# Context attention: the value products of the preceding chunk between the two halves of a slot

## The chip, the cores and the metric

The kernel runs on one core of a Trainium2 chip, in one launch. The metric is the device time in microseconds; of several runs the median is given. The core has five engines with an instruction queue each: PE (TensorE, the matmuls), ACT (ScalarE), DVE (VectorE), POOL (GpSimd) and SP (SyncE, which here only issues transfers). They meet through semaphores alone.

## The reference

A small transformer block on a batch of 2. `ctx` has 77 rows of 512 values, `x` has 2048; 16 heads of 32 values, relative position biases in every attention, layer norms with scale and bias:

```
mem = ctx + mha(ln(ctx), ln(ctx));   mem = mem + ffn(ln(mem))            # 77 rows, small
y = x + mha(ln1(x), ln1(x), causal + bias)                               # self attention, 2048 rows
y = y + mha(ln2(y), mem, bias)                                           # context attention: 2048 queries, 77 keys
out = y + relu(ln3(y) @ w1.T + b1) @ w2.T + b2                           # feed-forward, width 2048
```

with `mha = softmax(q k' / sqrt(32) + bias) v`, then an output projection. All is float32. The kernel splits the operands of the large products into a high and a low part and adds three products (high high, high low, low high).

## The kernel before, in words

The stages follow one another: projections and the small context part, self attention, its output with the context queries, **context attention** (`cross_attention`, line 1369), feed-forward (`feed_forward`). Each is a block with one program for each engine; the next begins when all engines have left it.

In context attention the 4096 tokens are 8 groups of 512 tokens. A **chunk** q is 4 heads (128 of the 512 query columns) of one group, so there are 32 chunks (NQ); `q // 4` is the group and `q % 4` the set of heads. A chunk has 4 tiles of 128 tokens; tile n is `4 q + i`. For a chunk the work is:

- `score(n)`, PE, line 1505: three matmuls, 128 queries by 4 x 77 keys, into one of three PSUM banks `ca_s`; it waits until the exponentials three tiles back are done. The first score of a chunk waits for the chunk's queries.
- `shift(n)`, DVE: the negated maximum of each head (`ca_ng`, line 1642), with a bias added first (line 1640) for a few tiles near the start of each batch.
- `exponent(n)`, ACT, line 1582: four exponentials into `ca_pq`; `sums(n)` (line 1647) and `inverse(n)` (line 1652, two tiles at once) on DVE; the normalising multiplication on POOL (line 1484), two tiles at a time.
- `turn(q, j)`, PE, line 1519: four transposes of head j into one of two banks `ca_t`; the first head waits for POOL's normalising of each of the four tiles. `evacuate(q, j)`, ACT, line 1590, copies them to `ca_pt`, of which there are two, by the chunk's parity.
- `values(q)`, PE, line 1528, operation `ca_o` of line 1533: the **value products**, four matmuls of 77 x 32 by 512 (eight in the profile) into the one bank `ov`. Two waits stand ahead of them: for the four copies of chunk q, and for `low(q - 1)`, which frees the bank.
- `high(q)`, ACT, line 1596 (written as `sa_q`, which lends its room), and `low(q)`, DVE, line 1657 (`sa_k`): the two parts of the result.
- `project(e, ...)`, PE, line 1537, operation `ca_p` of line 1547: the output projection of tile e (128 tokens, all heads) in two halves of six matmuls. The first half waits for `low` of all four chunks of the tile's group. `residual(e)`, DVE, line 1662, adds it to `y`, and SP stores `y`.

The order of the work is written out by hand: every engine walks through the same slots, q from -2 to 36. In **slot** q PE works on `turn` of chunk q, `score` of chunk q + 2, `project` of tile q - 5 and `values` of chunk q - 1. All but the last is in two halves. ACT does `high(q - 2)` first in a slot, then in each half two copies and two tiles' exponentials; DVE does `low(q - 2)` first, then in each half two shifts, two sums of the tiles before, an inverse, and in half 0 the residual of tile q - 6. As tile e is projected in slot e + 5, the first tile of a group (e = 4, 8, ...) comes in slots 9, 13, ..., and needs `low` of chunk e + 3, which DVE does in that same slot.

POOL, in slot q: two pairs of normalisings, the bias row added to a `y` tile (line 1491), and one piece of later weights loaded, rounded and split (lines 173, 179, 181); in slot 5 also a memset (line 1498). In slot 29 DVE does the statistics of the feed-forward stage's first layer norm ahead of its shifts (`head_stats`), and in slot 30 ACT its square root ahead of its copies; PE transposes the result at the end of slot 32 (`head_turn`).

PE's part of the slot in the kernel before:

```python
            for q in slots():
                e = q - LAG
                for half in range(2):
                    ...
                    if has(e, NE):
                        project(e, (2 * half, 2 * half + 1))
                if has(q - 1):
                    values(q - 1)
                if q == NQ:
                    head_turn()
```

Of the kernel before, what the change touches and what calls it, by code (L numbers as in the profile page):

```python
# [152 lines left out]
def waits(engine, sem, value):  # L153

    if not (isinstance(value, int) and value <= 0):
        engine.wait_ge(sem, value)
# [1212 lines left out]
def cross_attention(k, io, dr, ident, w, split, src, dst, early, pair, stored, w2):  # L1369
# [7 lines left out]
    with k:  # L1377
# [26 lines left out]
        def slots():  # L1404
            return range(-LEAD, NQ + LAG)

        def chunk(q):
            return q // KC, q % KC, q // KC // GB
# [8 lines left out]
        def has(q, count=NQ):  # L1417
            return 0 <= q < count
# [84 lines left out]
        @block.tensor  # L1503
        def _(pe):
            def score(n):
                q, i = n // TT, n % TT
                g, m, b = chunk(q)
                if i == 0:
                    waits(pe, s[f"q{q % QB}"], 16 * (q // QB + q % QB // 2))
                    if q == NQ // B:  # L1510
                        pe.wait_ge(s["key1"], 16 * 2 * HC)
                waits(pe, s["exp"], n - 2)
                t = slice(i * P, (i + 1) * P)
                for x, (a, c) in enumerate(((0, 0), (0, 1), (1, 0))):
                    last = pe.matmul(sps[n % 3][:, 0:W], qb[q % QB][:, a, t], kd[b][:, c, m, :],
                                     start=(x == 0), stop=(x == 2))
                last.then_inc(s["score"], 1)

            def turn(q, j):
                n = q * HC + j  # L1520
                waits(pe, s["copied"], n - 1)
                for i in range(TT):
                    if j == 0:
                        pe.wait_ge(s["normal"], TT * q + i + 1)
                    last = pe.transpose(tps[n % 2][0:S, i * P:(i + 1) * P], pq_rows[(TT * q + i) % (PB * TT)][:, j, :], ident[:])
                last.then_inc(s["turned"], 1)

            def values(q):
                g, m, b = chunk(q)
                pe.wait_ge(s["copied"], HC * (q + 1))  # L1530
                waits(pe, s["low"], q)
                for j in range(HC):
                    last = pe.matmul(ov[j * HD:(j + 1) * HD, :], cv[:, b, m * HC + j, 0:HD], pt[:, q % 2, j, :],
                                     start=True, stop=True)
                last.then_inc(s["value"], 1)

            def project(e, cs):
                g, i = e // TT, e % TT
                if cs[0] == 0:
                    if e == 0:  # L1540
                        pe.wait_ge(split.s["lo"], KC)
                    pe.wait_ge(s["low"], KC * (g + 1))
                    waits(pe, s["done"], e - 1)
                t = slice(i * P, (i + 1) * P)
                for c in cs:
                    for x, (a, ww) in enumerate(((oh, wo_h), (oh, wo_l), (ol, wo_h))):
                        last = pe.matmul(ops[e % 2][:], a[g % 2][:, c, t], ww[:, c, :],
                                         start=(c == 0 and x == 0), stop=(c == KC - 1 and x == 2))
                if cs[-1] == KC - 1:
                    last.then_inc(s["product"], 1)  # L1550

            def head_turn():
                pe.wait_ge(s["normed"], TT)
                for c in range(KC):
                    for i in range(TT):
                        last = pe.transpose(banks[c][:, i * P:(i + 1) * P], xn0[:, i, c * P:(c + 1) * P], ident[:])
                    last.then_inc(s["across"], 1)
# [4 lines that stand above are left out]
                    if has(q):  # L1562
                        for j in (2 * half, 2 * half + 1):
                            turn(q, j)
                    if has(q + LEAD):
                        for i in (2 * half, 2 * half + 1):
                            score(TT * (q + LEAD) + i)
                    if has(e, NE):
                        project(e, (2 * half, 2 * half + 1))
                if has(q - 1):  # L1570
                    values(q - 1)
                if q == NQ:
                    head_turn()

# [657 lines left out]
```

## Time and profile before

| | us |
|---|---|
| median of 3 runs | 2810.82 (2808.09 to 2813.54) |
| the profiled execution | 2810.91 |
| its span, first to last instruction | 2808.8 |
| context attention, PE's first score to its last projection | 1819.99 to 2078.6 |
| PE busy over the span | 2705.2 (96%) |
| mean granted clock of TensorE | 0.987 |

Times in the trace count from the span's start. PE, ACT, DVE and POOL are the engines' work; PEld is PE's loading of weights, which runs beside its matmuls. A row of a timeline gives the start, the time that the merged instructions take together, the engine, the line, the operation with the tiles that it writes and reads, how many there are, and in brackets the idle time of the engine before it with what ended it. A matmul's end is modelled, so two rows of PE may overlap by some tenths; starts are what to go by. Slot 24 starts at 2003.83, slot 5 at 1862.09 and slot 7 at 1878.32.

### The profile page before, as it was taken

To read this page: it belongs to the slowest core of one execution; us is meant where nothing else is said; L and a number is where in the kernel's file an instruction comes from. 1 tells how busy PE (TensorE), PEld (TensorE's weight loads), DVE (VectorE), ACT (ScalarE), POOL (GpSimd) and SP (SyncE) were. 2 spreads that over 40 slices of the span, in tenths; PEclk is the share of its full clock that TensorE was granted. 3 is DMA by queue.
4 is the path that set the end of the run, shared out by engine and by line. 5 is a ranking of instruction groups with operands and counts; after the bars stand their busy time and mean duration, and the time that the engine had idled before them with its cause. 6 is when DMAs were issued, how large, how long until landed. Compare 5 with 4: busy or idle time off the path is not lost. (4 is left out here: it accounts for less than half of the span.)

```text
span 2808.8 us, 40054 instructions
## 1 busy us (share of the span) xinstructions
PE 2705.2 (96%) x12704; PEld 1794.2 (64%) x12704; DVE 1602.1 (57%) x3851; ACT 1238.1 (44%) x2624; POOL 417.4 (15%) x497
## 2 busy tenths in 40 slices
PE   7999989999999999999999889889999999999998
PEld 6788854444444444444444378767778888888886
DVE  5554367777777777777777288567643222122211
ACT  2322114555555555555555433488843323332231
POOL 5000021000000000000000422088557000000000
PEclk9999988999999999999999999999999999999999
DMA  7656653222222222222222388455431000000000
GB/s 222 220 187 207 196 155 80 69 68 67 69 69 69 69 70 69 69 68 62 58 60 49 101 219 255 179 178 181 154 115 40 31 30 31 30 0 30 31 16 16
DMA packets 138949, 272.96 MB, mean 97 GB/s; under 512 B 24885, under 2 KB 56117, under 8 KB 133498
## 3 DMA queue, kind: packets, MB, share of 16 engines
q1 hardware_dynamic: 133530, 255.14, 31.5%
q0 software_dynamic: 5216, 15.33, 1.9%
q8 instruction: 101, 1.65, 0.2%
q14 instruction: 102, 0.84, 0.1%
HBM read 176.02 MB, written 99.98 MB: 98 GB/s over the span
## 5 line engine op out<-in xcount | busy, mean ns | idle before, releaser
L1277 ACT ACTIVATE sa_pr<-sa_st 128x512 f32<-128x512 f32 (+3 forms) x1280 | 611.0, 532 | 538.2 <-DVE sa_st L1340 294.7
L1243 PE MATMUL sa_ov<-sa_pr,sa_v 128*33 128x512 f32 (+3 forms) x2560 | 535.8, 540 | 0.0
L1324 DVE TENSOR_REDUCE sa_part<-sa_mp 128x1 f32<-128x512 f32 x760 | 408.3, 584 | 115.0 <-PE sa_mp L1222 114.4
L1232 PE MATMUL sa_st<-sa_q,sa_k 97*128 97x512 f32 (+3 forms) x1280 | 441.7, 413 | 18.2 <-ACT sa_pr L1277 13.7
L1232 PEld LDWEIGHTS sa_st<-sa_q,sa_k 97*128 97x128 f32 x1280 | 217.0, 190 | 319.7 <-ACT sa_pr L1277 214.3
L1222 PE MATMUL sa_mp<-sa_k,sa_q 96*128 96x512 f32 (+1 forms) x1256 | 362.3, 382 | 10.6 <-PEq L1204 5.5
L1321 DVE CUSTOM_DVE_ANT_0 sa_mp<-sa_mp,sa_ub 128x512 f32<-128x512 f32 (+1 forms) x496 | 308.4, 665 | 76.9 <-PE sa_mp L1222 75.0
L148 PE MATMUL ff_f<-sa_q,ff_w 128*128 128x512 f32 x1024 | 336.5, 390 | 2.9 <-PEq L2039 2.9
L2034 PE MATMUL ff_o<-ff_w,ca_q 128*128 128x512 f32 x1280 | 330.2, 392 | 3.6 <-DVE ca_q L2085 3.6
L2085 DVE TENSOR_TENSOR ca_q<-ca_v,ca_q 128x512 fp32r<-128x512 f32 x128 | 95.8, 749 | 379.5 <-ACT ca_q L2069 379.5
L1243 PEld LDWEIGHTS sa_ov<-sa_pr,sa_v 128*33 128x33 f32 x2560 | 122.2, 111 | 256.6 <-issue 208.2
L1222 PEld LDWEIGHTS sa_mp<-sa_k,sa_q 96*128 96x128 f32 x1256 | 225.9, 192 | 76.1 <-DVE sa_part L1324 23.3
L2034 PEld LDWEIGHTS ff_o<-ff_w,ca_q 128*128 128x128 f32 x1280 | 238.3, 188 | 55.2 <-DVE ca_q L2085 3.7
L2066 ACT ACTIVATE ca_v<-ff_f,ff_b 128x512 f32<-128x512 f32 x128 | 87.8, 686 | 381.7 <-PE ff_f L148 381.7
L1340 DVE TENSOR_TENSOR sa_st<-sa_st,sa_tb 128x256 f32<-128x256 f32 (+1 forms) x608 | 206.2, 381 | 75.6 <-PE sa_st L1232 74.2
L148 PEld LDWEIGHTS ff_f<-sa_q,ff_w 128*128 128x128 f32 x1024 | 192.3, 188 | 43.1 <-PEq L2039 3.3
L148 PE MATMUL ff_f<-sa_k,ff_w 128*128 128x512 f32 x512 | 199.5, 390 | 0.0
L1193 POOL TENSOR_TENSOR sao_ot<-sao_ot,sao_rb 128x512 f32<-128x512 f32 x8 | 10.2, 1272 | 1135.5 <-DMA sao_rb<-scratch_inv 1135.5
L1582 ACT ACTIVATE ca_pq<-ca_s,ca_ng 128x77 f32<-128x77 f32 x512 | 117.6, 342 | 21.9 <-DVE ca_ng L1642 21.7
L148 PEld LDWEIGHTS ff_f<-sa_k,ff_w 128*128 128x128 f32 x512 | 96.2, 188 | 19.9
L148 PE MATMUL qkv_ring<-sa_k,qkv_w 128*128 128x512 f32 x384 | 96.8, 405 | 4.4 <-DVE sa_k L271 3.6
L148 PE MATMUL sa_qps<-sa_ln_hi,ca_wq 128*128 128x512 f32 x256 | 87.8, 412 | 10.4 <-DVE sao_qst L1954 10.4
(239 smaller groups left out, 3283.7 us busy)
## 6 DMA issues: line engine op xcount, KB each, us to landing
sa_q<-scratch_q SPq DMA_DIRECT2D x96, 256.0 KB, 7.6
sa_k<-scratch_k SPq DMA_DIRECT2D x96, 256.0 KB, 8.6
scratch_q<-sao_qst SPq DMA_DIRECT2D x32, 512.0 KB, 4.2
ca_q<-scratch_q SPq DMA_DIRECT2D x32, 512.0 KB, 4.3
scratch_q<-sa_q SPq DMA_DIRECT2D x28, 512.0 KB, 7.8
scratch_k<-sa_q SPq DMA_DIRECT2D x28, 512.0 KB, 5.5
sa_v<-scratch_v SPq DMA_DIRECT2D x16, 528.0 KB, 13.5
scratch_o<-sa_osb SPq DMA_DIRECT2D x128, 66.0 KB
```

The lines of the kernel that those rows point to most:

```text
L148: last = pe.matmul(out, s, m, start=(k == 0), stop=(k == n - 1))
L1222: pe.matmul(mp[a % 2][:, h, 0:w], qs[n.par][rows, h, qb * P:(qb + 1) * P], ks[n.par][rows, h, k0:k0 + w], start=True, stop=True).then_inc( ...
L1232: pe.matmul(st[bank(u, h)][:, 0:w], ks[n.par][:, h, kb * P:(kb + 1) * P], qs[n.par][:, h, g * GW + c0:(g + 1) * GW], start=True, stop=True ...
L1243: last = pe.matmul(ov[64 * h:64 * h + VW, c0:GW], vs[n.par][:, kb, h, :], pr[:, u % 4, h, 0:GW - c0], start=(u in opens), stop=(u in ends))
L1277: act.activation(pr[:, u % 4, h, 0:w], st[bank(u, h)][:, 0:w], ACT.Exp, scale=SCALE).then_inc(s["exp"], 1)
L1321: dve.tensor_tensor_reduce(tile, tile, ub[n.par][:, h, GW - w:GW], 1.0, NEG, ALU.add, ALU.max, to)\
L1324: dve.tensor_reduce(to, tile, AX_X, ALU.max).then_inc(s["red"], 1)
L1340: dve.tensor_tensor(tile, tile, tb[n.par][:, h, t0:t0 + w], ALU.add).then_inc(s["bias"], 1)
L1582: last = act.activation(pq_rows[r][:, j, :], sps[n % 3][:, j * S:(j + 1) * S], ACT.Exp, bias=ng[:, r, j:j + 1])
L2034: last = pe.matmul(ops[i][:], a[:, f % 2, t], b[f], start=(f == 0 and n == 0), stop=(f == FC - 1 and n == 2))
L2066: act.activation(hf[:, f % 2, :], fps[f % 2][:], ACT.Relu, bias=b1[:, f:f + 1]).then_inc(s["relu"], 1)
L2085: dve.tensor_tensor(hl[:, f % 2, :], hf[:, f % 2, :], raw(hh[:, f % 2, :]), ALU.subtract)\
```

## The change

In PE's program of context attention, `values(q - 1)` stands inside the loop over the two halves, and is issued in half 0 alone, after that half's turns, scores and projection. The programs of the other engines, the waits and the instructions themselves are the same.

```diff
@@ -1567,8 +1567,8 @@
                             score(TT * (q + LEAD) + i)
                     if has(e, NE):
                         project(e, (2 * half, 2 * half + 1))
-                if has(q - 1):
-                    values(q - 1)
+                    if half == 0 and has(q - 1):
+                        values(q - 1)
                 if q == NQ:
                     head_turn()
```

## Rows read from the trace of the kernel before

**Rows 1.** The page, part 1: busy time of each engine, share, instructions.
```profile
PE 2705.2 (96%) x12704; PEld 1794.2 (64%) x12704; DVE 1602.1 (57%) x3851; ACT 1238.1 (44%) x2624; POOL 417.4 (15%) x497
```
**Rows 2.** The page, part 4: lines of the chain that ended last.
```profile
PE ff_o L2034 13%; PE ff_f L148 12%; PE ff_ln_tp L251 0%; DVE ff_y L2090 0%; DVE sa_v L2090 0%; DVE ca_q L2085 0%; DVEq L72 0%; DVEq L319 0%; PEldq L2039 0%; DVEq L2084 0%; DVEq L2089 0%; PEldq L2017 0%; PEldq L215 0%; PEldq L214 0%
```
**Rows 3.** Stretches: length, busy PE, PEld, DVE, ACT, POOL, then clock, DMA, GB/s.
```profile
1829.00:1834.00 5.00, 2.20 (x9) 1.91 (x10) 0.96 (x3) 2.31 (x9) 4.92 (x7) 0.50 0.95 339
...
1845.00:1862.00 17.00, 14.92 (x105) 10.35 (x105) 12.00 (x32) 16.47 (x59) 15.17 (x22) 1.00 0.42 132
...
1871.00:2041.00 170.00, 170.00 (x1109) 131.24 (x1108) 118.08 (x284) 144.86 (x484) 123.71 (x155) 1.00 0.52 166
```
**Rows 4.** Timeline of PE, slot 24 and the start of slot 25.
```profile
2003.83 1.10 PE L1525 MATMUL ca_t<-ident,ca_pq 128*77 128x128 f32 x8
...
2005.62 0.64 PE L1547 MATMUL ca_p<-ca_wo,sa_q 128*128 128x512 f32 x2
...
2007.02 1.03 PE L1525 MATMUL ca_t<-ident,ca_pq 128*77 128x128 f32 x8
2007.81 1.09 PE L1515 MATMUL ca_s<-ca_k,ca_q 128*128 128x308 f32 x6
...
2010.20 1.07 PE L1533 MATMUL ca_o<-ca_pt,ca_v 77*32 77x512 f32 x8
2011.20 0.99 PE L1525 MATMUL ca_t<-ident,ca_pq 128*77 128x128 f32 x7
```
**Rows 5.** Timeline of ACT in the same slot.
```profile
2009.03 1.83 ACT L1582 ACTIVATE ca_pq<-ca_s,ca_ng 128x77 f32<-128x77 f32 x8 [0.30 <-DVE ca_ng L1642]
2011.34 0.60 ACT L1596 ACTIVATE sa_q<-ca_o 128x512 fp32r<-128x512 f32 x1 [0.47 <-PE ca_o L1533]
```
**Rows 6.** Timeline of DVE in the same slot.
```profile
2008.52 0.90 DVE L1642 TENSOR_REDUCE ca_ng<-ca_s 128x4 f32<-128x308 f32 x2 [0.65 <-PE ca_s L1515]
...
2011.97 0.69 DVE L1657 TENSOR_TENSOR sa_k<-ca_o,sa_q 128x512 fp32r<-128x512 f32 x1 [1.55 <-ACT sa_q L1596]
```
**Rows 7.** Timeline of all engines, end of slot 4 and slot 5.
```profile
1862.07 1.84 ACT L1582 ACTIVATE ca_pq<-ca_s,ca_ng 128x77 f32<-128x77 f32 x8
...
1863.72 0.67 ACT L1596 ACTIVATE sa_q<-ca_o 128x512 fp32r<-128x512 f32 x1
...
1864.43 0.69 DVE L1657 TENSOR_TENSOR sa_k<-ca_o,sa_q 128x512 fp32r<-128x512 f32 x1 [1.75 <-ACT sa_q L1596]
...
1865.27 0.69 PE L1547 MATMUL ca_p<-ca_wo,sa_q 128*128 128x512 f32 x2 [1.22 <-DVE sa_k L1657]
```
**Rows 8.** Timeline of all engines, slots 3 and 4.
```profile
1852.25 0.69 DVE L1657 TENSOR_TENSOR sa_k<-ca_o,sa_q 128x512 fp32r<-128x512 f32 x1 [1.75 <-ACT sa_q L1596]
...
1852.75 1.15 PE L1525 MATMUL ca_t<-ident,ca_pq 128*77 128x128 f32 x8 [0.85 <-ACT ca_pt L1590]
...
1857.63 0.67 ACT L1596 ACTIVATE sa_q<-ca_o 128x512 fp32r<-128x512 f32 x1
```
**Rows 9.** Timeline of all engines, slots 5 to 7: POOL's queue and PE's turns.
```profile
1870.21 1.36 POOL L1484 TENSOR_TENSOR ca_pq<-ca_pq,ca_inv 128x308 f32<-128x308 f32 x2 [1.06 <-DVE ca_inv L1652]
...
1875.26 2.15 POOL L1498 MEMSET ca_k<- 128x2464 f32 x1
...
1877.38 2.66 POOL L1484 TENSOR_TENSOR ca_pq<-ca_pq,ca_inv 128x308 f32<-128x308 f32 x4
...
1878.32 1.23 PE L1525 MATMUL ca_t<-ident,ca_pq 128*77 128x128 f32 x8
```
**Rows 10.** Timeline of all engines, slots 15 and 16.
```profile
1942.01 1.36 POOL L1484 TENSOR_TENSOR ca_pq<-ca_pq,ca_inv 128x308 f32<-128x308 f32 x2
...
1944.77 1.10 PE L1525 MATMUL ca_t<-ident,ca_pq 128*77 128x128 f32 x8
```
**Rows 11.** Timeline of PE, slots 29 and 30.
```profile
2046.61 0.69 PE L1515 MATMUL ca_s<-ca_k,ca_q 128*128 128x308 f32 x3 [1.25 <-ACT ca_pq L1582]
...
2052.59 1.15 PE L1525 MATMUL ca_t<-ident,ca_pq 128*77 128x128 f32 x8 [0.52 <-ACT ca_pt L1590]
```

## Prediction

> **What bounds the kernel now.** First the page: PE is busy 96% of the span [rows 1], and the chain that ended last runs almost wholly over the feed-forward stage behind the changed one [rows 2]. Nothing of context attention is on it by name, but feed-forward begins only when PE has left context attention, so a microsecond won or lost there moves the end by one. Second, the stretches [rows 3]: from 1871 to 2041 us, slots 6 to 28, PE is busy 170.00 of 170.00 us, so it is the bound there and has no gap to fill. Ahead of that (1845 to 1862 us, slots 2 to 4, which have no projection yet) it is busy 14.92 of 17.00 us while ACT is busy 16.47: there ACT is the bound.
>
> Third, one slot in order of time. It starts with its first turn at 2003.83 and the next one starts at 2011.20, so it takes 7.37 us [rows 4]. Below, "at 3.2" means 3.2 us after a slot's start. The projection of half 0 starts at 1.79, the turns of half 1 at 3.19, the scores of half 1 at 3.98; the value products start at 6.37 and hold PE for 1.00 until 7.37. ACT and DVE work behind: ACT's exponentials of half 1 start at 5.20, and the next `high` starts at 0.14, having waited 0.47 for the value products [rows 5]; DVE's shift of half 1 starts at 4.69 after a wait for the scores and `low` starts at 0.77 [rows 6].
>
> **The change, part by part.** No instruction is added or removed: the same eight value matmuls stand after half 0 instead of after half 1. In a stretch where PE never waits, a new order of the same work costs 7.37 us a slot as before. What can change are waits. The products pass the turns, scores and projection of half 1, so those start 1.00 later after the slot's start, and so does what hangs on them: ACT's copies, DVE's shifts and inverses, POOL's normalising. SP's next query load waits for the scores of half 1; it comes 1.0 later for a chunk that is first read two slots (14.7 us) on, so it is covered. The store of the residual hangs on half 0.
>
> (a) Steady slots. With everything of half 1 later by 1.00, the exponentials start at 6.20. In slot 5, where ACT runs without pause, `high` starts 1.65 after the exponentials, `low` 0.71 after `high`, and a projection that waits for `low` starts 0.84 after `low` [rows 7]. So `high` starts at 6.20 + 1.65 - 7.37 = 0.48 (now 0.14: its wait of 0.47 takes up most of the delay) and `low` at 1.19 (now 0.77), done at 1.88. The moved products need that `low` only at 3.2: covered by 1.2 us. But the projection of the first tile of each group, in slots 9, 13, 17, 21, 25 and 29, needs `low` of the chunk two slots back and is reached at 1.79; it would start at 1.19 + 0.84 = 2.03, a stall of 0.24. Five of these six stand before the tail: 5 x 0.24 = +1.2 us; the sixth is in (d). Bounds: 0 if ACT catches up, and 5 x (0.77 + 1.00 + 0.84 - 1.79) = 5 x 0.82 = 4.1 if the whole 1.00 reaches `low`. I take 1.2, since ACT's own wait is in the row.
>
> (b) Slots 2 to 4, bound by ACT with a period of 6.09 (1857.63 to 1863.72) [rows 7, 8]. There PE waits 0.85 in mid-slot for ACT's copies, which looks like free room for the value products. But they need `low` of two chunks back: in slot 3 it runs 1852.25 to 1852.94, and the turns start at 1852.75 now [rows 8]. The products would start at 1852.25 + 0.84 = 1853.09 and the turns at 1854.09, 1.3 later. A ring closes: `low` to products 0.84, products 1.00, turns to scores 0.79, scores to shift 0.71, shift to exponentials 0.51, to `high` 1.65, to `low` 0.71 [rows 4 to 7]: 6.21 against 6.09, so 0.1 a slot, three slots: +0.3 us. Bounds: 0, and 3 x 1.3 = 4.0 if nothing takes up the later turns; the ring is near the lower one.
>
> (c) Slot 5 to 7, POOL. In slot 5 POOL's second pair of normalisings waits 1.06 for the inverse of half 1; then comes everything in one queue without a gap up to the memset of 2.15 us and the next pair at 1877.38, done at about 1878.72, while slot 7's first turns start at 1878.32 and their block takes 1.23, against 1.10 in the slot of rows 4 [rows 4, 9]. So POOL already is 0.1 late there. The inverse comes 1.00 later now, the whole row of POOL's work moves, and PE stalls: +1.0 us, once. Bounds 0 and 1.0; I take 1.0 because no wait lies in between to take it up. In other slots POOL has room: the tightest pair starts at 1942.01, takes 1.36, and is needed from 1944.77 on [rows 10]: 1.4 us of margin, 0.4 after the change.
>
> (d) The tail. In slot 29 PE waits 1.25 for an exponential that is late because DVE does the head's statistics first, and in slot 30 it waits 0.52 for ACT [rows 11]. The statistics follow `low`, so the exponential is later by 0.42 while the products now run before it: PE passes the point at 2046.61 + 0.42 with the 1.00 of products behind it, a gain of 0.6, with the sixth projection stall inside. The wait of slot 30 moves by the same 0.42, with its products behind it too, so it adds nothing. -0.6 us. Bounds: 0 and -1.25 - 0.52 = -1.8.
>
> **Sum.** 1.2 + 0.3 + 1.0 - 0.6 = +1.9 us. The profiled execution took 2810.91 us, 2.1 more than its span of 2808.8; the median of the three timed runs is 2810.82, the same within 0.1. 2810.9 + 1.9 = 2812.8 us. The bounds add up to -1.8 and +9.1 - so 2809 to 2820. In short: a move inside a saturated stretch, slightly for the worse at its seams. A measurement of this kernel can tell about 0.2%, 5.6 us, from no change.
>
> **The rivals.**
> 1. The products fill idle time. For it: PE's waits of 0.85 in slot 3, 1.22 in slot 5, 1.25 and 0.52 at the end [rows 7, 8, 11]; against it: those of slots 3 and 5 end with ACT's and DVE's chain, which the products don't shorten. If all four went and slot 4's was like slot 3's: -4.7, so 2806.2 us.
> 2. On the other side, the delay reaches `low` whole. Place: the projection of the group's first tile. It decides when ACT has no idle time to give; ACT waits 0.47 before `high` and 0.30 before the exponentials [rows 5], of which I count the first. Price: 4.1 for (a), 0.3, 1.0, and no gain in the tail: +5.4, so 2816.3 us; more if ACT falls so far back that the products in mid-slot wait as well, from `low` ending after 3.0.
> 3. The move does nothing measurable: the seams (b), (c) and the stalls of (a) are all taken up by waits that I didn't follow. 2810.9 us.
> 4. The clock. PE would now pause in slots 7, 9, 13 and so on where it did not. With waits of 0.85 in the stretch from 1845 to 1862 the granted clock stayed 1.00, which is 2.4 GHz; it was 0.50, which is 1.2 GHz, from 1829 to 1834, where PE was busy only 2.20 of 5.00 us [rows 3, 8]. One slot at the lower level would cost about as much again as it takes, +7.4, so 2820 us. The new pauses are at most 1.1 long, so I hold this unlikely. The Trainium skill, "TensorE: Matmul & The Clock Gate", section "A second HAM failure mode: psum-queue depth-cycling", says that frequent short pauses of PE between groups of matmuls can make the clock go to and fro; by that rule this rival would be the forecast, and the trace speaks against it in slots 2 to 4.
>
> **How the numbers follow.** Forecast (sum above, own range 2809 to 2816): 0.60. Rival 1: 0.07. Rival 2: 0.18. Rival 3: 0.12. Rival 4: 0.03. The range 2807.5 to 2819 reaches over rival 2 and to half of rival 1, and leaves out what is left of rivals 1 and 4 and the outer end of 2. Faster by over 0.2% (below 2805.2): about half of rival 1, 0.04. Slower by over 0.2% (above 2816.4): half of rival 2, rival 4, and a twentieth of the forecast: 0.15. Within: 0.81.
>
> **What would show it.** In the changed profile PE should still be busy all of its slots 8 to 28 but for waits of about 0.2 us of the projection for `low` in slots 9, 13, 17, 21 and 25; a slot should take 7.37; the turns of slot 7 should wait about 1.1 us for POOL; `high` should no longer wait for the value products and start near 0.48. The value products of slots 2 to 4 should wait for `low`. The wait in slot 29 should shrink from 1.25 to about 0.7. I am wrong if the value products wait in mid-slot in the steady slots, if the projection's waits are 0.8, or if a slot without any wait takes another time than 7.37, which would mean that the order itself has a price.

## The result, and the profile after

| | before | changed |
|---|---|---|
| median, us | 2809.64 (2804.12 to 2813.87, 20 runs) | 2813.85 (2806.72 to 2820.41, 20 runs) |
| ratio | | 1.0014, 95% interval 1.0007 to 1.0020 |
| profiled execution: span, us | 2808.8 | 2810.4 |

So the change costs 3.9 us, between 2.0 and 5.6 by the interval. The forecast was +1.9 us and 2812.8 us, with 2807.5 to 2819 as its range.

A span is too coarse for this: in these two executions the stages ahead differ by 3 us by themselves (context attention's first score at 1819.99 and at 1817.02). What the change does is read from marks on PE within the stage. These five stretches follow one another from the first score to feed-forward's first matmul:

| stretch, us | before | changed | difference | forecast |
|---|---|---|---|---|
| first score to the first turn that POOL releases | 11.65 | 12.36 | +0.7 | none |
| to the first projection (slots 0 to 5) | 33.63 | 34.89 | +1.3 | +0.3 |
| to slot 8 | 20.55 | 21.75 | +1.2 | +1.0 |
| slots 8 to 28 | 154.90 | 156.88 | +2.0 | +1.2 |
| slot 29 to feed-forward | 40.76 | 40.04 | -0.7 | -0.6 |

The first stretch has no value products at all; over the profiles of this study it goes from 10.8 to 12.5 with the products at the end of the slot and from 11.4 to 12.4 with them in mid-slot, so its 0.7 is not the change's. The other four make +3.7.

The page after, part 1, answers to [rows 1]: the same counts, the same 96%.

```profile
PE 2704.3 (96%) x12704; PEld 1793.7 (64%) x12704; DVE 1600.4 (57%) x3851; ACT 1235.5 (44%) x2624; POOL 416.6 (15%) x497
```

Two views of stretches of the changed kernel (columns as in [rows 3]). The saturated stretch of 170.00 us now has PE busy 168.69; and there is something that the kernel before does not show in these slots, a granted clock of 0.50 (1.2 GHz) from 1853 to 1856.

```profile
1871.00:2041.00 170.00, 168.69 (x1088) 128.54 (x1087) 113.96 (x279) 139.49 (x475) 122.83 (x154) 1.00 0.52 165
```
```profile
1845.00:1851.00 6.00, 4.53 (x36) 3.45 (x29) 4.03 (x11) 5.95 (x21) 4.48 (x7) 1.00 0.45 129
...
1853.00:1856.00 3.00, 3.00 (x15) 2.99 (x14) 1.40 (x4) 2.31 (x9) 1.45 (x3) 0.50 0.01 3
```

Half 1 of slot 24 and slot 25 of the changed kernel, all engines; this answers to [rows 4 to 6]. The value products now stand between the halves; 2001.43 to 2008.81 is one slot without a wait, 7.38 us as before.

```profile
2001.43 1.07 PE L1533 MATMUL ca_o<-ca_pt,ca_v 77*32 77x512 f32 x8
...
2005.59 1.04 PE L1525 MATMUL ca_t<-ident,ca_pq 128*77 128x128 f32 x8
...
2008.81 1.06 PE L1533 MATMUL ca_o<-ca_pt,ca_v 77*32 77x512 f32 x8
...
2009.81 1.10 PE L1525 MATMUL ca_t<-ident,ca_pq 128*77 128x128 f32 x8
...
2010.50 1.08 ACT L1590 ACTIVATE ca_pt<-ca_t 77x512 f32<-77x512 f32 x2 [0.71 <-PE ca_t L1525]
...
2011.37 0.90 DVE L1642 TENSOR_REDUCE ca_ng<-ca_s 128x4 f32<-128x308 f32 x2 [1.49 <-PE ca_s L1515]
...
2011.88 1.83 ACT L1582 ACTIVATE ca_pq<-ca_s,ca_ng 128x77 f32<-128x77 f32 x8 [0.30 <-DVE ca_ng L1642]
...
2013.00 1.03 PE L1525 MATMUL ca_t<-ident,ca_pq 128*77 128x128 f32 x8
...
2013.55 0.65 ACT L1596 ACTIVATE sa_q<-ca_o 128x512 fp32r<-128x512 f32 x1
...
2014.24 0.69 DVE L1657 TENSOR_TENSOR sa_k<-ca_o,sa_q 128x512 fp32r<-128x512 f32 x1 [0.96 <-ACT sa_q L1596]
...
2014.98 0.19 PEld L1547 LDWEIGHTS ca_p<-ca_wo,sa_q 128*128 128x128 f32 x1 [0.35 <-DVE sa_k L1657]
```

The reader is to see three things. `high` (2013.55) no longer has a wait for the value products in brackets: it starts 0.55 after the slot, behind its own exponentials. ACT's wait has moved to its copies, 0.71 for the turns, because those stand behind the value products. And the projection of the group's first tile waits for `low`, in weight loads: 0.35. A list of the waits of PE's weight loads, 1880 to 2044 us, shows that this is all that is new there (us in total, times, longest):

```profile
PEld ca_p L1547 <- DVE sa_k L1657: 1.7, 5, 0.3
```

PE alone at that place shows the price. The projection starts 1.19 after the scores, 0.26 later than the 0.93 or so without a wait, and its second row follows after 0.58 instead of 0.47. The slot is 7.73 to 7.76 long, 0.37 more than the 7.38 that the others take on average.

```profile
2013.79 1.10 PE L1515 MATMUL ca_s<-ca_k,ca_q 128*128 128x308 f32 x6
2014.98 0.74 PE L1547 MATMUL ca_p<-ca_wo,sa_q 128*128 128x512 f32 x2
2015.56 0.40 PE L1547 MATMUL ca_p<-ca_wo,sa_k 128*128 128x512 f32 x1
```

The second part, 0.11, goes with the weight load. In half 0 of slot 24, where nothing waits, the load starts 0.14 ahead of its matmul; behind the wait both start at 2014.98. Nearly the same step, 0.56, stands in the tail at 2065.72, where the projection follows the value products without a wait for another engine and its load again starts with it. So it is the load that isn't ahead, and not the wait, that goes with the late second step.

```profile
2011.45 0.33 PEld L1547 LDWEIGHTS ca_p<-ca_wo,sa_q 128*128 128x128 f32 x2
2011.59 0.64 PE L1547 MATMUL ca_p<-ca_wo,sa_q 128*128 128x512 f32 x2
...
2012.07 0.40 PE L1547 MATMUL ca_p<-ca_wo,sa_k 128*128 128x512 f32 x1
...
2065.72 0.30 PEld L1547 LDWEIGHTS ca_p<-ca_wo,sa_q 128*128 128x128 f32 x2 [0.84 <-issue]
2065.72 0.73 PE L1547 MATMUL ca_p<-ca_wo,sa_q 128*128 128x512 f32 x2
...
2066.28 0.39 PE L1547 MATMUL ca_p<-ca_wo,sa_k 128*128 128x512 f32 x1
```

Slots 2 and 3, PE, answering to [rows 8]. The value products wait 0.37 for `low` in slot 2 and 1.48 in slot 3, and behind those of slot 3 the same blocks as in every slot take nearly twice their time: scores to turns 1.69 (1853.15 to 1854.84) where 0.94 (1846.59 to 1847.53) is usual.

```profile
1844.74 1.06 PE L1533 MATMUL ca_o<-ca_pt,ca_v 77*32 77x512 f32 x8 [0.37 <-DVE sa_k L1657]
...
1846.59 1.10 PE L1515 MATMUL ca_s<-ca_k,ca_q 128*128 128x308 f32 x6
1847.53 1.14 PE L1525 MATMUL ca_t<-ident,ca_pq 128*77 128x128 f32 x8
1848.43 1.10 PE L1515 MATMUL ca_s<-ca_k,ca_q 128*128 128x308 f32 x6
1851.01 1.07 PE L1533 MATMUL ca_o<-ca_pt,ca_v 77*32 77x512 f32 x8 [1.48 <-DVE sa_k L1657]
1852.00 1.49 PE L1525 MATMUL ca_t<-ident,ca_pq 128*77 128x128 f32 x8
1853.15 1.89 PE L1515 MATMUL ca_s<-ca_k,ca_q 128*128 128x308 f32 x6
1854.84 1.60 PE L1525 MATMUL ca_t<-ident,ca_pq 128*77 128x128 f32 x8
```

Slots 5 to 7, all engines, answering to [rows 9]: POOL's pair starts after 1.42 of idle time, where it was 1.06. Counted from the first projection (1864.27 here, 1865.27 before) the pair, the memset and the next pair all start 1.15 or 1.16 later than before, and slot 7's turns wait for it, 0.50 and 0.32; in the kernel before their block took 0.13 longer than usual.

```profile
1870.36 1.36 POOL L1484 TENSOR_TENSOR ca_pq<-ca_pq,ca_inv 128x308 f32<-128x308 f32 x2 [1.42 <-DVE ca_inv L1652]
...
1875.42 2.15 POOL L1498 MEMSET ca_k<- 128x2464 f32 x1
...
1877.40 0.38 PE L1525 MATMUL ca_t<-ident,ca_pq 128*77 128x128 f32 x2
...
1877.53 2.67 POOL L1484 TENSOR_TENSOR ca_pq<-ca_pq,ca_inv 128x308 f32<-128x308 f32 x4
...
1878.29 0.33 PE L1525 MATMUL ca_t<-ident,ca_pq 128*77 128x128 f32 x1 [0.50 <-POOL ca_pq L1484]
...
1878.94 0.77 PE L1525 MATMUL ca_t<-ident,ca_pq 128*77 128x128 f32 x5 [0.32 <-POOL ca_pq L1484]
```

The tail, PE, answering to [rows 11]: slot 29's wait has shrunk from 1.25 to 0.28, slot 30's of 0.52 has become one of the value products of 0.46.

```profile
2049.25 0.70 PE L1515 MATMUL ca_s<-ca_k,ca_q 128*128 128x308 f32 x3 [0.28 <-ACT ca_pq L1582]
...
2054.05 1.07 PE L1533 MATMUL ca_o<-ca_pt,ca_v 77*32 77x512 f32 x8 [0.46 <-DVE sa_k L1657]
```

### The profile page after: what moved, and what is told of

Same layout as the page of the kernel before. It is cut to its first block and busy times, and to the rows that moved or that the text cites. A ratio compares the mean times of both kernels' runs of the same rounds, so it can differ in the third digit from the quotient of the medians.

```text
span 2810.4 us, 40054 instructions
## 1 busy us (share of the span) xinstructions
PE 2704.3 (96%) x12704; PEld 1793.7 (64%) x12704; DVE 1600.4 (57%) x3851; ACT 1235.5 (44%) x2624; POOL 416.6 (15%) x497
## 5 line engine op out<-in xcount | busy, mean ns | idle before, releaser
L1193 POOL TENSOR_TENSOR sao_ot<-sao_ot,sao_rb 128x512 f32<-128x512 f32 x8 | 10.2, 1273 | 1132.5 <-DMA sao_rb<-scratch_inv 1132.5
```

## The experiments

All experiments compute the whole reference. The four stretches from the table above, in us, for every profile, with the timed ratio to the kernel before where there is one:

| run | to first projection | to slot 8 | slots 8 to 28 | slot 29 on | ratio (95%) |
|---|---|---|---|---|---|
| before | 33.63 | 20.55 | 154.90 | 40.76 | 1 |
| changed | 34.89 | 21.75 | 156.88 | 40.04 | 1.0014 (1.0007 to 1.0020) |
| e1_mid_from_8 | 33.71 | 20.57 | 157.00 | 40.08 | 1.0012 (1.0003 to 1.0021) |
| e2_mid_to_7 | 34.14 | 21.75 | 154.84 | 40.76 | 1.0013 (1.0004 to 1.0022) |
| e3_end_in_4th | 35.04 | 21.77 | 154.86 | 39.60 | 1.0000 (0.9991 to 1.0009) |
| e4_changed_again | 34.14 | 21.76 | 156.87 | 40.04 | 1.0015 (1.0005 to 1.0025) |
| e5_changed_memset4 | 34.12 | 20.50 | 156.88 | 40.03 | 1.0007 (0.9995 to 1.0018) |
| e6_before_memset4 | 33.63 | 20.38 | 154.90 | 40.74 | 0.9997 (0.9988 to 1.0006) |
| e7_mid_from_29 | 33.71 | 20.40 | 154.89 | 39.78 | 0.9994 (0.9982 to 1.0005) |
| e8_seams_out | 33.72 | 20.50 | 154.90 | 39.60 | 0.9995 (0.9985 to 1.0005) |
| e9_changed_clock_a | 35.33 | 21.76 | 156.88 | 40.04 | |
| e10_changed_clock_b | 34.18 | 21.78 | 156.92 | 40.08 | |
| e11_mid_1_to_4 | 34.86 | 20.53 | 154.89 | 40.77 | |
| e12_before_clock | 33.72 | 20.54 | 154.90 | 40.94 | |

Between runs that have the same order in a stretch it repeats within 0.15 us, but for the first column, on which see the clock below, and two of the last: in e7 and e12 the step from the last projection to feed-forward took 3.06 and 3.07 instead of 2.89.

**Where in the stage.** Two kernels that make the move in a part of the slots only.

```diff
-                    if half == 0 and has(q - 1):
+                    if half == (0 if q >= 8 else 1) and has(q - 1):     # e1; e2 has q < 8
```

> Value products in mid-slot from slot 8 on, at the end of the slot in slots 1 to 7. Yardsticks of the two profiles so far: from the first projection matmul to slot 8, 20.6 us before and 21.8 changed; from slot 8 to slot 29, 154.9 and 156.9; from slot 29 to the first matmul of feed-forward, 40.8 and 40.0. Theory (the seams: projection's wait for low in every fourth slot, POOL's memset, the slots bound by ACT, the tail): 20.6, 156.9, 40.0; time +1.2 us over before. Rival (the order costs something in every slot): slots without a wait longer than 7.38. Rival (all of it is the start): time as before, 154.9.

> Value products in mid-slot in slots 1 to 7 only. Theory of the seams: slots 2 to 4 wait in mid-slot for low (33.6 becomes 34 to 35 us from PE's first waited-for turn to the first projection), POOL's memset makes the turns of slot 7 wait 0.8 us or more (21.8), then 154.9 and 40.8 as before; time +1.4 to +2.4 us, the upper end if the clock falls in slot 2 as it did in the changed profile. Rival (the first slots only move waits about): 33.6, 20.6, time +0.

Each kernel has the changed kernel's value in the stretches where it makes the move and the value of before in the others (e2's 34.14 is the changed kernel's value in those of its profiles in which the clock does not fall). So the four terms are independent of each other and add. Without them the slots are 7.38 on average, as before; the rivals of a price in each slot and of an effect of the start alone fall. The timed runs (+3.4 us for e1, +3.7 for e2) agree in sign, and each is above its sum of stretches (1.5 and 1.7), though inside the interval. Differences of a microsecond are for the trace; the timed ratio can't carry them.

**The projection's wait for `low`.** The changed kernel, with the last chunk of each group put back to the end of its slot.

```diff
-                    if half == 0 and has(q - 1):
+                    if half == (0 if not (q % 4 == 0 and 8 <= q <= 28) else 1) and has(q - 1):
```

> The changed kernel, but in slots 8, 12, ..., 28 the value products stand at the end of the slot again, so that the last chunk of a group is not later at low. Theory: the projection's waits for low in slots 9, 13, ..., 29 go, slot 8 to slot 29 falls from 156.9 to 154.9 (the slot length is 7.38 in all), time -1.9 us against the changed kernel. Rival (the order has its own price in each slot, the fourth slot is long for another reason): 155.5 to 156.9.

The stretch falls from 156.88 to 154.86, and PE's weight loads have no wait for `low` any more in the list of waits (1871 to 2050 us; all of it):

```profile
PEld ca_t L1525 <- issue: 20.1, 24, 0.8
PEld ca_o L1533 <- issue: 8.6, 24, 0.4
PEld ca_t L1525 <- POOL ca_pq L1484: 1.2, 2, 0.7
```

That settles the largest term, 2.0 us: five waits that lengthen their slots by 0.37 each, and 0.1 to 0.2 spread over the slots between. The tail gains 0.4 too (40.04 to 39.60), but not from the sixth stall, in slot 29: behind that one PE still waits 0.28 in the changed kernel, which takes the stall up. What comes earlier in e3 is the exponential that this later wait is for: the scores behind it start 5.89 after the slot's start, as in the kernel before, and 6.35 in the changed one, since there `low` and the statistics behind it are late. In time the kernel is at 1.0000, against 1.0014 of the changed one.

**POOL's memset.** The memset of the second batch's keys in four pieces, one each in slots 6 to 9, and their load moved to slot 10; once on the changed kernel, once on the kernel before.

```diff
-                if q == LAG:
-                    pool.memset(raw(kd[1][:]), 0.0).then_inc(s["zero1"], 1)
+                if 6 <= q < 10:
+                    pool.memset(raw(kd[1][:, (q - 6) // 2, 2 * (q % 2):2 * (q % 2) + 2, :]), 0.0).then_inc(s["zero1"], 1)
...
-                sp.wait_ge(s["zero1"], 1)
+                sp.wait_ge(s["zero1"], 4)
...
-                if q == LAG + 1:
+                if q == 10:
                     load_k(1)
```

> The changed kernel with POOL's memset of the second batch's keys (2.15 us in slot 5) cut into four, one in each of slots 6 to 9, and the load that needs it moved from slot 6 to slot 10. Theory: POOL has 0.85 us to spare in a slot, so a quarter of 0.54 delays nothing; slot 7's turns no longer wait, from the first projection to slot 8 it takes 20.5 us instead of 21.8; time -1.3 us against the changed kernel. Rival (POOL is late through the value products alone, not through the memset): 21.5 or more, and slots 8 and 9 grow.

> The same cut of the memset in the kernel before. Theory: there POOL was late by 0.13 us only; 20.55 becomes 20.4, time -0.1 us, not to be told from before. Rival (the memset costs the kernel before too): -1 us.

The changed kernel goes from 21.76 to 20.50, the kernel before from 20.55 to 20.38. So of the 1.2 us 1.09 is the memset meeting a later inverse; the last 0.12 is the order's own around slot 5. PE's turns of slot 7 on the changed kernel with the memset in four no longer wait, and POOL again has idle time before its pair:

```profile
1873.34 1.03 PE L1525 MATMUL ca_t<-ident,ca_pq 128*77 128x128 f32 x8
```
```profile
1873.70 1.36 POOL L1484 TENSOR_TENSOR ca_pq<-ca_pq,ca_inv 128x308 f32<-128x308 f32 x2 [0.98 <-DVE ca_inv L1652]
```

**The seams taken out.** First the only place where the move gains, then the move nearly everywhere in the saturated stretch, both with the memset in four.

```diff
+                    if half == (0 if q >= 29 else 1) and has(q - 1):                                     # e7
+                    if half == (0 if q >= 5 and not (q % 4 == 0 and q <= 28) else 1) and has(q - 1):     # e8
```

> The kernel before with the memset in four and the value products in mid-slot from slot 29 on. Theory: 33.6, 20.4, 154.9, and from slot 29 to feed-forward 39.6 instead of 40.8, as in the run where slot 28 has them at the end; time -1.3 us against before, 0.05%, hardly to be told in the timed runs. Rival (the tail's gain is eaten by the value products waiting for low in slot 30): 40.0 or more.

> Value products in mid-slot from slot 5 on except in slots 8, 12, ..., 28, and the memset in four: the move in nearly all of the saturated stretch without its four seams. Theory: 33.6, 20.4, 154.9, 39.6, as the run that has them there from slot 29 on; time -1.3 us against before. Rival (the order has a price of its own, which the seams hid): 155.5 or more from slot 8 to slot 29.

Both have the sum that was expected. e8 makes the move in 18 of the slots 5 to 28 and its 170 us from 1873 are as full as those of before:

```profile
1873.00:2043.00 170.00, 170.00 (x1109) 131.29 (x1108) 116.33 (x285) 143.43 (x487) 125.02 (x159) 1.00 0.53 167
```

In these slots the order itself has no price and no gain. The four stretches add up to 248.8 in e7 and 248.7 in e8, against 249.8 before and 253.6 changed. e7 and e8 are ahead of the changed kernel; 1 us ahead of the kernel before is shown by the trace only, as both intervals hold 1. By the stretches, what the tail gains is nearly all that there is to gain from this order.

**The clock.** The changed kernel for a second profile, then twice more; the move in slots 1 to 4 alone; and the kernel before again.

```diff
-                    if half == 0 and has(q - 1):
+                    if half == (0 if 1 <= q <= 4 else 1) and has(q - 1):     # e11
```

> The changed kernel once more, for a second profile. Theory: from slot 5 on the same within 0.2 us (21.8, 156.9, 40.0). The clock: in the first profile it fell to 0.50 for 3 us in slot 3 after PE's mid-slot wait of 1.48 in slot 2. If that belongs to the change it is seen again, if it is a matter of the execution it may be missing; the start (34.9 us) is then 1 to 1.5 us shorter. Time +2 to +5 us over before.

> The changed kernel, one more profile, for the clock alone. Of the five profiles so far with the products in mid-slot in slots 2 to 4, two show the granted clock at 0.50 in slot 3 (slot 3 takes 7.3 or 7.4 us instead of 6.27), of the five with them at the end none. Theory (the mid-slot waits of 1.5 us put PE near where the clock falls, and it depends on the execution): falls in some. Rival (those two were something else): in none of three.

> As the run before it: the changed kernel, for the clock in slots 2 to 4.

> The products in mid-slot in slots 1 to 4 alone. From PE's first waited-for turn to the first projection 34.1 us if the clock stays and about 34.9 if it falls, against 33.6 to 33.7; from there on everything as before: 20.55, 154.9, 40.8, the memset's late turns included, since slot 5's products are back at its end.

> The kernel before, for the clock: 1.00 in slots 2 to 4 by both theories, 33.6 us from the first waited-for turn to the first projection.

With the products in mid-slot in slots 2 to 4 the first column is 34.12 to 34.18 in four profiles, and 34.86, 34.89, 35.04 and 35.33 in the four others (changed, e3, e9, e11), where slot 3 alone takes 7.3 to 7.8 instead of 6.27. With the products at the end it is 33.63 to 33.72 in all six profiles. e4 is the changed kernel with the clock up: the wait of 1.47 is the same (it is in slot 3, as that of 1.48; e4's expectation puts it in slot 2), and the blocks behind it have their usual time.

```profile
1852.78 1.07 PE L1533 MATMUL ca_o<-ca_pt,ca_v 77*32 77x512 f32 x8 [1.47 <-DVE sa_k L1657]
1853.78 1.10 PE L1525 MATMUL ca_t<-ident,ca_pq 128*77 128x128 f32 x8
1854.63 1.09 PE L1515 MATMUL ca_s<-ca_k,ca_q 128*128 128x308 f32 x6
1855.56 0.49 PE L1525 MATMUL ca_t<-ident,ca_pq 128*77 128x128 f32 x3
```
```profile
1846.78:1852.78 6.00, 4.53 (x36) 3.44 (x29) 4.03 (x11) 5.96 (x21) 4.50 (x7) 1.00 0.44 128
...
1853.00:1856.00 3.00, 3.00 (x25) 2.04 (x17) 2.03 (x7) 2.92 (x11) 2.92 (x4) 1.00 0.33 91
```

So the move brings two costs to slots 2 to 4: 0.45 us always, and in half of the executions 0.7 to 1.2 more from a fall of the clock. Four of eight against none of six points to the waits in mid-slot as its cause but does not prove it: if the order played no part, all four falls would be among these eight profiles in 7 cases of 100. What decides between executions of the same kernel stays open. The waits don't tell them apart: slot 3's is 1.46 to 1.49 in all eight, slot 2's is 0.36 to 0.59 in the four that fall and 0.69 to 0.90 in the others, and in the 6 us ahead of slot 3's products PE is busy 4.5 us in all eight. One difference stands at the start of the stage, where the clock is low in every profile: for 17.1 us in the four that fall, but also in e10, which doesn't, and for 10.2 to 13.7 us in e2, e4 and e5. e11 also shows the start alone: all its other stretches are as before.

## Why the prediction was right or wrong

The measured +3.9 us (2.0 to 5.6) has the sign of the forecast's +1.9 and lies in its range; the same outcome, within 0.2% of before, was the likeliest. The mechanism held but for the clock: no price in a slot of the saturated stretch (e8), and costs at the seams that it named. Its sum was half of what was measured; the largest part of what is missing is term (a), the next the fall of the clock. By its steps:

- **(a) Steady slots.** Right in place and cause (e3). `high` was put at 0.48 after the slot's start and came at 0.55, `low` at 1.19 and came at 1.24. The term was mis-sized: 5 x 0.24 = 1.2 against 2.0 measured. Two things were missing. The turns at the start of a slot no longer stand behind the value products and take 0.79 instead of 0.86, so the projection is reached 0.07 sooner; and where its weight load isn't ahead, PE loses another 0.11. A third was wrong the other way: from `low` to the projection that waits for it it is 0.74 (2014.24 to 2014.98) and not the 0.84 of slot 5. So the start of the projection moves by 0.26, near the forecast's 0.24, by errors that cancel, and each of the five slots is 0.37 longer. The first could have been read in rows of before: 0.79 is the step from 2007.02 to 2007.81 in [rows 4].
- **(b) Slots 2 to 4.** The ring was put at 6.21 us and measures 6.25 to 6.28, and the three slots cost 0.45 against 0.3. What failed is the working of rival 4: I held the new pauses to be at most 1.1 long, and gave a fall of the clock 0.03. The working of (b) itself has the products start at 1853.09 when PE is ready for them before 1852, a wait of more than 1.1, and I did not carry it over. The clock fell in half of the profiles, at 0.7 to 1.2 us and not at 7.4, because it is down for 3 us and not for a slot, and a part is won back behind it: slot 4 then takes 5.95 to 5.97 instead of 6.27. The Trainium skill's rule that frequent short pauses make the clock go to and fro ("TensorE: Matmul & The Clock Gate", "A second HAM failure mode: psum-queue depth-cycling") is borne out here in part: in four profiles of eight it falls once and comes back, 1.1 to 1.6 us after the end of slot 3's wait of 1.5, and in none of the six with waits of 0.85 to 0.93 in slots 3 and 4 [rows 8].
- **(c) The memset.** +1.0 forecast, 1.09 by e5 and e6 and 1.2 in all.
- **(d) The tail.** -0.6 forecast, -0.7 measured. The exponential came 0.46 later (0.42 forecast), and slot 29 is 0.6 shorter. Its wait was to become 0.7 and became 0.28: the 0.7 is 1.25 + 0.42 - 1.00, from which the sixth stall of the projection, 0.37, was still to be taken off. The sum is right all the same, as the wait ends with the exponential whether PE stalls before it or not.
- **Rivals.** Rival 1 (idle time filled) gives the sign wrong: the mid-slot waits were not filled but grew where the clock stayed up, from 0.9 to 1.47 in slot 3 and to 1.15 in slot 4, because `low` ends them. Rival 2 (the whole delay reaches `low`) is refused by `low` at 1.24 and not at 1.77. Rival 3 (nothing) is refused by the interval, and by those of e1, e2 and e4, which leave out 1 too.

The four terms as measured make 0.45 + 1.2 + 2.0 - 0.7 = +3.0, or +3.4 with half of a clock fall of 0.9. That is inside the interval of the timed runs.

## What to carry to other kernels

In a stretch where the bound engine is never idle, moving its work about gained nothing here (e8), however much idle time stands elsewhere in the stage; look at the seams, where another engine's queue sets a wait, and count every step that the move puts behind the moved work. Give work that depends on the moved one its slack in the same units: here 0.2 us of slack behind `low` was all that the projection had, while the moved products had 1.2 and POOL's tightest pair 1.4. Where an edit makes an engine pause longer, work out how long the pause is, not only how much time it costs.

## What the runs showed of the hardware that was not expected

- The clock can fall from 2.4 to 1.2 GHz in the middle of a stage, 1.1 to 1.6 us after the end of a wait of PE of 1.5 us, with no longer wait in slots 1 to 3; it did so in four of eight profiles with that wait and came back within 4 us. At the low level weight loads filled 2.99 of 3.00 us, against 2.04 in e4 with the clock up. PE was busy 4.53 of 6.00 us ahead of the fall, and as much in e4, where there was none.
- Where the first weight load of a chain of matmuls starts with its matmul and not 0.14 us ahead of it, the second row came 0.09 to 0.11 us late (0.56 or 0.58 instead of 0.47): behind a wait of 0.35 for another engine, and behind value products without such a wait. So a wait can cost more than its length.
- Turns of eight transposes that follow the value products (32 columns of weights) take 0.86 us to the next block, those that follow the projection 0.79, wherever in the slot they stand (2009.81 to 2010.66, and 2013.00 to 2013.79).
